# Weights requested ahead of the norms, eight norm tiles in flight, and keys turned sooner in a two-block network on one Trainium2 core

## The chip, the cores and the metric

One core of a Trainium2 chip runs the whole network in one program, in float32. The metric is the device time of one execution in microseconds, on the slowest core, which here is the only one. An execution's time is its profiled span and the start and end around it.

## The reference

x has 2 sequences of 2048 tokens and 128 channels. Four sublayers follow, each with a residual and a layer norm over the channels behind it:

```python
x = _layernorm(x + gated_delta(x))      # first mixer: 16 heads, keys 64 wide, values 128 wide
x = _layernorm(x + ffn_block(x))        # two layers of local attention and a gated feed forward
x = _layernorm(x + wkv_mixer(x))        # second mixer
x = _layernorm(x + ffn_block(x))

# inside the first mixer
q, k, v = (silu(causal_conv(x @ w, conv)) for w, conv in ...)      # 4 taps
q, k = q * rsqrt(sum(q * q) + 1e-6), k * rsqrt(sum(k * k) + 1e-6)  # per head
g = -exp(A_log) * softplus(x @ w_a + dt_bias);  beta = 2 * sigmoid(x @ w_b)
S = S * exp(g_t);  delta = (v_t - k_t @ S) * beta_t;  S = S + outer(k_t, delta);  o_t = (q_t / 8) @ S
y = o * rsqrt(mean(o * o) + eps) * norm_w * silu(x @ w_g);  return y @ w_out

# inside a layer of ffn_block
x = x + local_attention(rope(l2norm(q) * q_scale), rope(l2norm(k) * k_scale), v) @ wo
h = layernorm(shift_token(x)) * ln_g + ln_b
x = x + ((h @ w1a + b1a) * gelu(h @ w1g + b1g)) @ w2 + b2
```

## The kernel before

Activations lie with channels on the partitions, in three buffers (x0T, x1T, x2T), a sequence beside the other, each with 3 columns of zeros ahead. The program is a row of phases. Each phase is one or more blocks (`nc.Block()`): within one, every engine has its own instruction stream and waits on semaphores; at its end all engines, SyncE's stream too, come together. `phase_semaphores` clears a phase's semaphores on GpSimd in a block of its own, with lines at L83.

**gated_delta** (L150) takes a sequence in 16 chunks of 128 tokens, so 32 turns. A turn has named parts on each engine. `early`: projection of a and b, then projections 0 to 3 (the keys in 0 and 1, the queries in 2 and 3), 4 taps each, into PSUM banks 4 and 5 in turn; ScalarE copies each out with Silu (L491). VectorE does the scalar chain of the decays, `decays` (L570 to L585), and `norms`: sums of the squares that GpSimd made (L717), the multiplication by the inverse norms (L602) that GpSimd's power made (L724). GpSimd makes gV, four tiles (L720), as input to the cumulated log decays (TensorE L359). `mid`: sums and logs of the decays, then for the keys and after that the queries: eight turns through TensorE (L367), ScalarE's copy (L508), the 16 heads' products (L375). VectorE makes nA from the key products (L612), PT from the query products (L616). SyncE carries the diagonal blocks of nA to DRAM and back, VectorE inverts them, SyncE carries the inverses into Tm (L317 to L325). `late`: projections 4 to 7 (v), 8 to 11 (gate), products with the state, then three levels that merge the inverses (L381 turns Tm, L419 and L428), delta, output and state. `tail` turns y (L457) and projects it out (L463) into bank 7, and VectorE adds it to x (L684). Each engine runs these parts in the order `late(n)`, `early(n + 1)`, `tail(n)`, `mid(n + 1)`; each turn on TensorE ends with the products and the next begins with `early`.

**post_norm** (L1425) goes through the sequences in four rounds of two tiles of 128 x 512: sum or copy (L1484, L1486), mean by a product with ones (L1451), centring (L1489), squares (L1469), variance by one-column products (L1456), its scale (L1492), power on GpSimd (L1476), spreading (L1461), product (L1495). There are two PSUM banks for each of the two tiles.

**ffn_block** (L855) primes its semaphores (L831), loads the masks (L877) and copies them on GpSimd (L882), and runs both layers in a loop of the program: a block with 22 DMA requests of SyncE (L890 to L905), the multiplication of the rope table on VectorE (L916) and TensorE's wait for all weights; `attention_layer`; `feed_forward`. `build` runs post_norm, then copy_all (L2178), a copy of the normed activations for the residual, then ffn_block.

## Time and profile before

| | us |
|---|---|
| median of 3 runs (lowest, highest) | 6176.56 (6173.99, 6180.19) |
| the profiled execution | 6176.74 |
| its span | 6174.9 |
| TensorE busy | 5260.5 (85%) |
| VectorE busy | 3993.2 (65%) |
| ScalarE busy | 2818.8 (46%) |
| GpSimd busy | 2189.4 (35%) |
| mean granted TensorE clock | 0.911 of full |

The first mixer's turns run from about 67 to 3122 us, the first block from 3200 to 4134, the second mixer from 4187 to 5107, the second block from 5184 to 6110. Busy times overlap, since the engines run side by side; a releaser behind an idle time is what ended it. A clock of 1.00 is 2.4 GHz on TensorE, 0.50 is 1.2 GHz.

### The profile page before, as it was taken

The page shows a single profiled execution, that of the slowest core. Times are in us where ns is not written, and L with a number is a line of the kernel's source. Part 1 is how long each engine was busy: PE and PEld are TensorE (multiplying, and loading weights), DVE is VectorE, ACT ScalarE, POOL GpSimd, SP SyncE. Part 2 cuts the span into 40 slices and gives each one's busy share as a digit, 9 for nine tenths or more (in the row PEclk, how much of TensorE's full clock was granted, in tenths as well). Part 3 has the DMA queues.
Part 4 walks back from the last instruction along what each step waited for, and adds up shares of the span by engine and source line. Part 5 has one row for each costly group of instructions (what it writes and reads, how often), then busy time and mean ns, then how long its engine had stood idle before and what let it go on. Part 6 is the DMA issues. An engine that isn't in the chain of part 4 may idle for free. (4 is left out here: it accounts for less than half of the span.)

```text
span 6174.9 us, 107736 instructions
## 1 busy us (share of the span) xinstructions
PE 5260.5 (85%) x36898; PEld 3652.1 (59%) x36898; DVE 3993.2 (65%) x8920; ACT 2818.8 (46%) x6592; POOL 2189.4 (35%) x1545
## 2 busy tenths in 40 slices
PE   5999999999899999999959979985478775987988
PEld 3676776776667767667646635652156663654655
DVE  4655655556556565565549949944699545985983
ACT  1444444444444444344438838833400113874882
POOL 1323324333233233332326616603422113652650
PEclk7999999999999999999979989986699757998997
DMA  2000000000000000000000000000000000000000
GB/s 103 5 5 7 4 7 7 3 7 7 5 7 3 7 7 3 7 5 5 7 26 0 0 25 0 0 0 5 0 7 1 0 0 26 0 0 25 0 0 14
DMA packets 181374, 52.74 MB, mean 9 GB/s; under 512 B 151876, under 2 KB 177433, under 8 KB 180377
## 3 DMA queue, kind: packets, MB, share of 16 engines
q1 hardware_dynamic: 179880, 49.26, 3.5%
q10 hardware_dynamic: 1392, 2.20, 0.1%
q8 instruction: 55, 0.90, 0.1%
q14 instruction: 47, 0.38, 0.0%
HBM read 40.93 MB, written 10.49 MB: 8 GB/s over the span
## 5 line engine op out<-in xcount | busy, mean ns | idle before, releaser
L342 PE MATMUL gd_ps<-gd_taps,gd_xwin 128*128 128x512 f32 x2048 | 913.6, 605 | 0.0
L342 PEld LDWEIGHTS gd_ps<-gd_taps,gd_xwin 128*128 128x128 f32 x2048 | 391.9, 194 | 475.1 <-issue 472.9
L745 POOL TENSOR_TENSOR gd_o_rn<-gd_tmp,gd_mhalf 128x8 f32<-128x8 f32 x64 | 103.5, 1635 | 1189.8 <-DVE gd_tmp L670 1189.8
L522 ACT ACTIVATE gd_X<-gd_ps 128x512 f32<-128x512 f32 x512 | 267.8, 635 | 538.4 <-PE gd_ps L381 538.4
L1185 ACT ACTIVATE L_ffn_s<-L_ffn_s,L_ffn_nb,L_ffn_r 128x128 f32<-128x128 f32 x1024 | 408.0, 480 | 3.2
L647 DVE TENSOR_TENSOR gd_Z<-gd_ps,cst 128x256 f32<-128x256 f32 x384 | 163.1, 425 | 323.6 <-PE gd_ps L419 257.6
L1007 POOL TENSOR_TENSOR L_ffn_t<-L_ffn_t 128x512 f32<-128x512 f32 x128 | 162.4, 1268 | 541.5 <-DVE L_ffn_t L1224 541.5
L739 POOL TENSOR_TENSOR gd_gate<-gd_gate,gd_norm_w 128x2048 f32<-128x2048 f32 x32 | 145.1, 4535 | 588.1 <-ACT gd_gate L491 588.1
L491 ACT ACTIVATE gd_v<-gd_ps 128x512 f32<-128x512 f32 x128 | 76.4, 597 | 530.9 <-PE gd_ps L342 530.9
L381 PE MATMUL gd_ps<-cst,gd_gV 128*128 128x128 f32 x2048 | 269.6, 277 | 46.5 <-ACT gd_decay L517 46.5
L641 DVE SCALAR_TENSOR_TENSOR gd_v<-gd_ps,gd_n_ec,gd_v 128x128 f32<-128x128 f32 x512 | 135.2, 342 | 230.7 <-PE gd_ps L393 230.7
L1032 PE MATMUL L_ffn_ps<-L_ffn_sb_wqkv,L_ffn_hT 128*128 128x512 f32 x256 | 153.8, 684 | 144.5 <-ACT L_ffn_hT L1141 144.5
L381 PEld LDWEIGHTS gd_ps<-cst,gd_gV 128*128 128x128 f32 x2048 | 223.4, 142 | 77.6 <-ACT gd_decay L517 75.4
L602 DVE TENSOR_TENSOR gd_qk<-gd_qk,gd_r_norm 128x1024 f32<-128x1024 f32 x64 | 112.2, 1753 | 207.7 <-POOL gd_r_norm L724 207.7
L428 PE MATMUL gd_ps<-gd_Z,gd_X 128*128 128x64 f32 x2048 | 239.2, 275 | 0.0
L419 PE MATMUL gd_ps<-gd_gV,gd_nA 128*128 128x64 f32 x2048 | 235.8, 274 | 0.0
L428 PEld LDWEIGHTS gd_ps<-gd_Z,gd_X 128*128 128x128 f32 x2048 | 233.8, 192 | 0.0
L419 PEld LDWEIGHTS gd_ps<-gd_gV,gd_nA 128*128 128x128 f32 x2048 | 233.7, 192 | 0.0
L1016 POOL TENSOR_TENSOR L_ffn_r<-L_ffn_ss,L_ffn_mhalf 128x8 f32<-128x8 f32 x128 | 210.9, 1648 | 23.6 <-DVE L_ffn_ss L1256 23.6
L1075 PEld LDWEIGHTS L_ffn_ps<-L_ffn_kT,L_ffn_qT 64*64 64x64 f32 (+1 forms) x4096 | 149.0, 137 | 115.8 <-issue 100.9
L1086 PE MATMUL L_ffn_ps<-cst,L_ffn_s 128*128 128x128 f32 x1024 | 167.1, 286 | 58.4 <-ACT L_ffn_s L1185 58.4
L717 POOL TENSOR_TENSOR gd_scratch<-gd_qk 128x1024 f32<-128x1024 f32 x64 | 124.4, 1944 | 258.8 <-ACT gd_qk L491 258.8
(361 smaller groups left out, 13813.5 us busy)
## 6 DMA issues: line engine op xcount, KB each, us to landing
L_ffn_sb_rope<-in_rope SPq DMA_DIRECT2D x4, 2048.0 KB, 8.2
gd_tap_row<-in_L_attn_conv_v SPq DMA_DIRECT2D x2, 2048.0 KB, 6.8
gd_blocks<-gd_nA SPq DMA_DIRECT2D x256, 16.0 KB, 1.7
gd_Z<-gd_blocks SPq DMA_DIRECT2D x32, 128.0 KB, 2.0
gd_inverses<-gd_Z SPq DMA_DIRECT2D x32, 128.0 KB, 1.7
gd_gV<-gd_inverses SPq DMA_DIRECT2D x256, 16.0 KB, 1.9
L_ffn_sb_wqkv<-in_L_ffn_wqkv SPq DMA_DIRECT2D x4, 768.0 KB
gd_tap_row<-in_L_attn_conv_q SPq DMA_DIRECT2D x1, 2048.0 KB, 15.1
```

The costliest lines, as they stand in the source:

```text
L342: ins = pe.matmul(ps[4 + i % 2][:], xwin[:, t:t + P] if i < 8 else xwin[:, PAD:PAD + P], taps[:, t, 512 * SLICE[i]:512 * (SLICE[i] + 1)] i ...
L381: ins = pe.transpose(ps[4 + gi][:, P * k:P * (k + 1)], Tm[:, HG * gi + k], ident)
L419: ins = pe.matmul(ps[gi][:, 64 * k:64 * (k + 1)], nA[:, h], even(Tm, h, h + 1, s)[:, 0], start=True, stop=True)
L428: ins = pe.matmul(ps[gi][:, 64 * k:64 * (k + 1)], X[:, h], Z[:, h], start=True, stop=True)
L522: act.activation(heads(X, gi).rearrange("p h x -> p (h x)"), ps[4 + gi][:], ACT.Copy).then_inc(x_s.sem, 1)
L647: dve.tensor_tensor(heads(Z, gi), ps[gi][:, 0:256].rearrange("p (h x) -> p h x", h=HG), mask, ALU.mult).then_inc(z_s.sem, 1)
L1007: pool.tensor_tensor(t1[b][:, K], t1[b][:, K], t2[b][:, K], ALU.add).then_inc(la.k_sum.sem, 1)
L1016: pool.tensor_tensor(rq, ss[b][:, 0:AH], mhalf[:, 0:AH], ALU.pow).then_inc(la.r_q.sem, 1)
L1032: pe.matmul(ps_k[:], hT[b][:], wqkv[:, INNER:2 * INNER], start=True, stop=True).then_inc(la.k_mm.sem, 1)
L1075: ins = pe.matmul(ps_s[i][rows, P * k:P * (k + 1)], qT[b][half(i), k, rows], kT[b][half(i), k, WIN * wd:WIN * wd + P], start=True, stop=True)
L1086: ins = pe.transpose(ps_p[i][:, P * k:P * (k + 1)], s[b][:, i, k], ident)
L1185: ins = act.activation(s[b][:, i, k], s[b][:, i, k], ACT.Exp, scale=r[b][:, h:h + 1], bias=nb[b][:, i, k:k + 1])
```

## The change

In gated_delta TensorE turns the keys ahead of the decay sums, between the halves of the output's projection, and takes projection 4 between the query turns and the query products. ScalarE copies the keys ahead of the decays' exponentials. VectorE sums the key squares ahead of the decays and multiplies the keys ahead of the query sums. GpSimd takes the key power ahead of the query squares, the query power behind gV. In ffn_block the loads of layer 0 stand in a block ahead of the post norm, which is now called from within; the layer loop is unrolled; the next layer's rope, scales, wqkv and wo are requested in a block ahead of feed_forward, its w1, w2 and vectors beside the rope multiplication. post_norm has no loop: eight tiles, one PSUM bank each, all waits constants; it makes its constant and zeroes the pads on GpSimd, and ScalarE copies each finished tile to the second buffer where copy_all did.

```diff
@@ gated_delta, TensorE
+                def turn_qk(n, part):
+                    w((kn_s if part else qn_s).now(n))
+                    for q in range(2):
...
+                        w(proj_out.now(n, 2 + q) if m < 2 else t_out.now(n, q))
...
                 def late(n, b):
-                    for i in range(4, 12):
+                    for i in range(5, 12):
                         project(n, i)
...
+                def tail_and_mid(n):
+                    turn_y(n)
+                    output(n, range(0, G // 2))
+                    turn_qk(n + 1, 1)
+                    decay_sums(n + 1)
+                    output(n, range(G // 2, G))
+                    k_products(n + 1, 1)
+                    turn_qk(n + 1, 0)
+                    project(n + 1, 4)
+                    k_products(n + 1, 0)
@@ gated_delta, ScalarE
                 def mid(n):
+                    copy_qk(n, 1)
                     w(c_mm.now(n)); w(S_s.before(n))
                     act.activation(e_c[:], ps[6][:, 0:2 * H], ACT.Exp).then_inc(c_s.sem, 1)
...
+                    copy_qk(n, 0)
@@ gated_delta, VectorE
+                def norms_and_decays(n):
                     cn.start(n)
...
+                    square_sums(n, 0)
+                    decays(n)
+                    normed(n, 0)
+                    square_sums(n, 1)
                     cn.end()
...
+                    normed(n, 1)
@@ gated_delta, GpSimd
                 def early(n):
...
+                    squares_of(n, 0)
+                    inverse_norms(n, 0)
+                    squares_of(n, 1)
                     w(g_s.now(n))
...
+                    inverse_norms(n, 1)
@@ ffn_block
         with nc.Block() as block:
             @block.sync
             def _(sp):
+                load_attention(sp, 0)
                 sp.dma_start(masks[:, 0:2], A["masks"]).then_inc(la.f_const, 16)
...
+                load_feed_forward(sp, 0)
+
+        meanwhile()
+        la.prime(nc)
...
+        for layer in range(DEPTH):
+            with nc.Block() as block:
...
+                @block.sync
+                def _(sp):
+                    if layer:
+                        load_feed_forward(sp, layer)
...
+                    pe.wait_ge(la.w_loaded, (layer + 1) * (16 * 2))
...
+                    dve.tensor_tensor(rope[:], rope[:], scales[:].unsqueeze(1).to_broadcast([P, NC, 4, AD]), ALU.mult)
+
+            attention_layer(nc, cst, xo, xa, la, masks, rope, wqkv, wo, ps, layer * NC, f"{pre}{layer}")
 
             with nc.Block() as block:
                 @block.sync
                 def _(sp):
...
+                    if layer + 1 < DEPTH:
+                        load_attention(sp, layer + 1)
+                    sp.wait_ge(la.f_loaded, (layer + 1) * (16 * 13))
+
+            feed_forward(nc, cst, xa, xo, la, w1, w2, vecs, L, layer * (T // FW), f"{pre}{layer}")
@@ post_norm
+                for i in range(n):
+                    pe.wait_ge(summed, i + 1)
+                    pe.matmul(ps[i][:], ones, x[i][:], start=True, stop=True).then_inc(mean, 1)
+                for i in range(n):
+                    pe.wait_ge(squares, i + 1)
...
+                if also is not None:
+                    for i in range(n):
+                        act.wait_ge(done, i + 1)
+                        act.activation(also[:, at(i)], dst[:, at(i)], ACT.Copy)
@@ build
-            post_norm(nc, cst, [x1], x1, sems, "n1_")
         x2 = flat(activations("x2T"))
-        copy_all(nc, x2, x1)
         with phase_semaphores(nc) as sems:
-            ffn_block(nc, A, cst, "L0_ffn_", x2, x0, sems)
+            ffn_block(nc, A, cst, "L0_ffn_", x2, x0, sems, lambda: post_norm(nc, cst, [x1], x1, sems, "n1_", x2, [x2]))
```

`load_attention` requests the rope table, six rows of scales, wqkv and wo: 9 DMAs. `load_feed_forward` requests w1, w2 in three, and 9 vectors: 13 DMAs. `turn_y`, `output`, `decay_sums` and `k_products` hold the instructions of the old `tail` and `mid`.

## Rows read from the trace of the kernel before

**Rows 1.** Busy time by stretch: span, then each engine's, granted clock, DMA share, GB/s.

```profile
1041.80:1054.70 12.90, 8.34 (x81) 7.21 (x80) 10.09 (x22) 4.05 (x6) 12.90 (x11) 0.81 0.04 4
```

**Rows 2.** Timeline of one turn on TensorE: start, us, operation, tiles, idle before and releaser.

```profile
1018.64 13.98 PE L342 MATMUL gd_ps<-gd_taps,gd_xwin 128*128 128x512 f32 x32
...
1034.21 3.74 PE L463 MATMUL gd_ps<-gd_X,gd_w_out 128*128 128x128 f32 x32
...
1043.47 1.09 PE L367 MATMUL gd_ps<-cst,gd_qk 128*128 128x128 f32 x8 [1.64 <-DVE gd_qk L602]
1044.81 2.06 PE L375 MATMUL gd_ps<-gd_kT 64*128 64x128 f32 x32 [0.25 <-ACT gd_kT L508]
...
1050.62 4.15 PE L375 MATMUL gd_ps<-gd_qT,gd_kT 64*128 64x128 f32 x32 [2.22 <-DVE gd_nA L612]
1054.70 14.97 PE L342 MATMUL gd_ps<-gd_taps,gd_xwin 128*128 128x512 f32 x32
...
1077.40 0.66 PE L381 MATMUL gd_ps<-cst,gd_gV 128*128 128x128 f32 x4 [0.33 <-ACT gd_decay L517]
```

**Rows 3.** Timeline of the same turn, VectorE.

```profile
1021.01 0.18 DVE L564 COPY gd_e_ab<-gd_ab 128x16 f32<-128x16 f32 x1
...
1026.64 1.87 DVE L570 TENSOR_SCALAR gd_tmp<-gd_e_ab 128x16 f32<-128x16 f32 x1
...
1044.97 2.28 DVE L602 TENSOR_TENSOR gd_qk<-gd_qk,gd_r_norm 128x1024 f32<-128x1024 f32 x1 [1.64 <-POOL gd_r_norm L724]
...
1048.33 4.21 DVE L612 SCALAR_TENSOR_TENSOR gd_nA<-gd_ps,gd_n_beta,gd_decay 128x128 f32<-128x128 f32 x16
```

**Rows 4.** Timeline of GpSimd, the same turn and the next.

```profile
1020.76 3.23 POOL L745 TENSOR_TENSOR gd_o_rn<-gd_tmp,gd_mhalf 128x8 f32<-128x8 f32 x2 [37.17 <-DVE gd_tmp L670]
1026.47 2.00 POOL L717 TENSOR_TENSOR gd_scratch<-gd_qk 128x1024 f32<-128x1024 f32 x1 [2.48 <-ACT gd_qk L491]
...
1035.19 4.03 POOL L720 TENSOR_TENSOR gd_gV<-gd_g,cst 128x512 f32<-128x512 f32 x4
1039.18 5.76 POOL L724 TENSOR_TENSOR gd_r_norm<-gd_sq_sum,gd_mhalf 128x16 f32<-128x16 f32 x2
...
1134.36 5.76 POOL L724 TENSOR_TENSOR gd_r_norm<-gd_sq_sum,gd_mhalf 128x16 f32<-128x16 f32 x2
```

**Rows 5.** Timeline of SyncE's DMA requests, same turn; line L325 by itself, its landing times.

```profile
1068.44 3.75 SPq L325 DMA_DIRECT2D gd_gV<-gd_inverses  x8
...
DMA to landing us min/median/max: 1.7/1.9/3.1
```

**Rows 6.** Busy time by stretch: clock behind nA, and in the second mixer.

```profile
1050.60:1056.60 6.00, 5.98 (x35) 4.49 (x36) 4.72 (x13) 0.00 (x0) 4.29 (x6) 0.50 0.21 19
4506.50:4509.30 2.80, 0.00 (x0) 0.00 (x0) 2.80 (x4) 0.00 (x0) 0.00 (x0) 1.00 0.00 0
```

**Rows 7.** Stretches of norm 1 and norm 2, then norm 2's timeline.

```profile
3122.40:3162.20 39.80, 30.70 (x144) 22.82 (x144) 15.19 (x33) 5.04 (x8) 7.96 (x8) 0.79 0.00 0
...
4134.60:4181.80 47.20, 39.40 (x144) 28.09 (x144) 17.32 (x33) 5.04 (x8) 8.05 (x8) 0.58 0.00 0
...
4136.14 3.78 PE L1451 MATMUL n_ps<-n_x,cst 128*128 128x512 f32 x4 [2.86 <-DVE n_x L1484]
...
4143.10 3.76 PE L1461 MATMUL n_ps<-cst,n_rstd 128*128 128x128 f32 x16
```

**Rows 8.** Timeline of seams: into block one, between its layers; second mixer's loads.

```profile
3176.82 0.41 SPq L890 DMA_DIRECT2D L_ffn_sb_rope<-in_rope  x1
...
3189.22 4.42 DVE L916 TENSOR_TENSOR L_ffn_sb_rope<-L_ffn_sb_rope,L_ffn_sb_scales 128x4096 f32<-128x4096 f32 x1 [19.33 <-DMA L_ffn_sb_scales<-in_L_ffn_k_scale]
...
3200.14 2.07 PE L1032 MATMUL L_ffn_ps<-L_ffn_sb_wqkv,L_ffn_hT 128*128 128x512 f32 x2 [38.69 <-ACT L_ffn_hT L1141]
...
3679.14 2.07 PE L1032 MATMUL L_ffn_ps<-L_ffn_sb_wqkv,L_ffn_hT 128*128 128x512 f32 x2 [23.74 <-ACT L_ffn_hT L1141]
...
4197.53 1.85 SPq L1594 DMA_DIRECT2D wf_vec<-in_L_attn_time_maa  x4
```

More of the change, by code:

```diff
@@ L351, in early, with k_products, decay_sums @@
                         project(n, i)
-                def mid(n):
+                def turn_qk(n, part):
+                    w((kn_s if part else qn_s).now(n))
+                    for q in range(2):
+                        m = 2 * (1 - part) + q
+                        w(proj_out.now(n, 2 + q) if m < 2 else t_out.now(n, q))
+                        for k in range(4):
+                            first = H * part + 8 * q + 2 * k
+                            ins = pe.transpose(ps[4 + q][:, P * k:P * (k + 1)], qk[:, first:first + 2].rearrange("p h x -> p (h x)"), ident)
+                        ins.then_inc(t_mm.sem, 1)
+                def k_products(n, part):
+                    for g0 in range(0, G, 2):
+                        w(t_out.now(n, 2 * (1 - part) + g0 // 2))
+                        w(exp_s.now(n, g0 + 1) if part else nA_s.now(n, g0 + 1))
+                        for k in range(HG):
+                            for gi in (g0, g0 + 1):
+                                at = pair(HG * gi + k)
+                                ins = pe.matmul(bank(gi)[:, k], kT[half(gi), at], (kT if part else qT)[half(gi), at], start=True, stop=True)
+                                if k == HG - 1:
+                                    ins.then_inc((kk_mm if part else kq_mm).sem, 1)
+                def decay_sums(n):
                     w(g_s.now(n))
@@ L458, in tail, with output @@
                         ins.then_inc(yt_mm.sem, 1)
-                    for gi in range(G):
+                def output(n, groups):
+                    for gi in groups:
                         w(yT_s.now(n, gi))
@@ L689, in _ @@
                     early(b * NC)
-                    decays(b * NC)
-                    norms(b * NC)
+                    norms_and_decays(b * NC)
                     mid(b * NC)
@@ L888, in _ @@
+        la.prime(nc)
+        ps = [ctx.enter_context(nc.psum_tensor(f"{pre}ps{i}", [P, 512], F32)) for i in range(8)]
+        L = [ps[0:4], ps[4:8]]
+        for layer in range(DEPTH):
+            with nc.Block() as block:
+                @block.gpsimd
+                def _(pool):
+                    if layer == 0:
+                        pool.wait_ge(la.f_const, 16)
+                        pool.tensor_copy(masks[:, 2:NC], masks[:, 1:2].to_broadcast([P, NC - 2, P]))
                 @block.sync
@@ new lines, in _ @@
+                for i in range(n):
+                    pe.wait_ge(squares, i + 1)
+                    for j in range(FW // P):
+                        ins = pe.matmul(ps[i][:, j:j + 1], sq[i][:, P * j:P * (j + 1)], ones[:, 0:1], start=True, stop=True)
+                    ins.then_inc(var_mm, 1)
+                for i in range(n):
+                    pe.wait_ge(rstd_s, i + 1)
+                    for j in range(FW // P):
+                        ins = pe.matmul(ps[i][:, P * j:P * (j + 1)], rstd[i][:, j:j + 1].to_broadcast([P, P]), ident, start=True, stop=True)
+                    ins.then_inc(spread, 1)
@@ L1498 @@
+                for i in range(n):
+                    dve.wait_ge(var_mm, i + 1)
+                    dve.tensor_scalar(var[i][:], ps[i][:, 0:FW // P], 1.0 / D, EPS, ALU.mult, ALU.add).then_inc(var_s, 1)
+                for i in range(n):
+                    dve.wait_ge(spread, i + 1)
+                    dve.tensor_tensor(dst[:, at(i)], ps[i][:], x[i][:], ALU.mult).then_inc(done, 1)
 RH, RS = 16, 8
```

236 lines of the change are left out of this document (91 added, 145 removed).

## The prediction

> **What bounds the kernel now.** Read first the busy times of the page, then the stretches. TensorE is busy 85% of the span, but no engine fills it, so each stage is read for what its last wait is. About half the span is the first mixer: 32 turns, one every 95.18 us (GpSimd's power for the inverse norms starts at 1039.18 and again at 1134.36 [rows 4]). I set T = 0 where a turn's projections begin on TensorE, 1018.4. Nearly everything in a turn is TensorE back to back; its stops stand together, between T 23.4 and T 36.3: 1.64 us for the normed keys, 0.25 for their copy, a short one for the normed queries, 2.22 for nA [rows 2], and the products behind nA take 4.15 us where the same 32 matmuls took 2.06 [rows 2]. In the 12.9 us of that stretch TensorE is busy 8.34, at a granted clock of 0.81 of full [rows 1]: the clock fell to 0.50 in the stop for nA and stayed there 6 us into the work behind it [rows 6]. That is why the projections behind it take 14.97 us where the ones of the turn's start took 13.98 [rows 2]. Outside the mixer the waste is at the seams: the four post norms last 39.8 to 47.2 us each for some 8 us of power on GpSimd and 15 to 17 of VectorE [rows 7], and between a norm and the first attention matmul TensorE stands 38.69 us (some 6 less in the second block, with fewer semaphores to clear), between the two layers of a block 23.74 [rows 8].
>
> **The first mixer, walked once through with the new order.** All starts are from rows; full clock is assumed first.
> VectorE and GpSimd, keys: the second key projection is out at T 8.0, since GpSimd's squares begin at T 8.07 and take 2.0 [rows 4], to T 10.1. VectorE, done with the gated output at 8.24, sums them (1.22) and adds, to 11.5. GpSimd's power takes 2.9 (5.76 for two [rows 4]), to 14.5. Meanwhile VectorE runs the decay chain. It took 5.8 from 1026.64: 19 instructions of some 0.2 us, and ahead of them L570 with 1.87 where a copy of the same size took 0.18; it ended with GpSimd's squares (1028.5) [rows 3, 4]. Without that it is 4.1 us; but its last two small instructions now meet the query squares on GpSimd (14.9 to 16.9) and the first gV tile (1.0 [rows 4]), so I take its end at T 18.0. The keys' multiplication then meets the next gV tile: 2.28 us like the one of row 1044.97 [rows 3], to T 20.3. Today the keys are there at T 24.9.
> TensorE: projections to 14.0, y turned to 15.8, half of the output 1.8 (half of 3.74 [rows 2]), to 17.6. It waits for the keys to T 20.4, 2.8 us: longer than today's 1.64. Then key turn 1.1, sums 0.6, logs 3.7 (8 of the 512-column matmuls, whose 32 took 13.98), second half of the output 1.8, key products 1.9: T 29.3. Query turn to 30.4, a copy, **project 4** 3.4 (13.98 / 4), to 34.1, query products 2.0, to T 36.1. Today TensorE is at T 36.3 then, without project 4. So 7 projections less: the rest, from 1054.70 to 1077.07 (1077.40 less its 0.33) less 3.43 and less the 1.0 lost to the clock, is 17.9, and the level 0 turn could start at T 54.3 instead of 59.0 [rows 2].
> What is late next is the **round trip of the inverse**. nA: query sums 1.2 plus a wait for a gV tile, power to 25.4, queries multiplied to 27.9 (2.28 again), output added, n_ec behind a GpSimd tile to 29.1, nA 4.21 [rows 3], to T 33.3 against 34.1 today. From its end to the last block's landing it is 21.5 us today (nA ends 1052.5 [rows 3]; its last DMAs are requested by 1068.44 + 3.75 and land 1.9 later [rows 5]). That gives T 54.8, so it, not TensorE, sets the start: 54.9 against 59.0, a gain of 4.1 us a turn. Project 4, moved into the wait for nA, thus earns nothing beyond what nA's own earliness allows; ahead of it stand only TensorE's own products, and ScalarE copies v in the same order as before.
> Clock: the new stop of 2.8 us is one piece with full work on both sides. In the second mixer a like stop of 2.8 us held 1.00 all through; today's 2.22 behind the shorter ones ends at 0.50 [rows 6]. If it drops, key turn, sums and logs run some 6 us at half clock, 2.8 us are lost, the key products and nA slip to T 35.4, and the gain is 1.9. I take the middle of the two, 3.0, since the rows show one case that held and one that didn't: 30 turns x 3.0 = 90. The first turn of each sequence has no output to put in between and its decays now wait behind the key squares; project 4 fills the wait for nA: 3 us each, 6. Sum **96**; bounds 30 x 1.9 and 30 x 4.1, so 60 to 130.
>
> The Trainium skill, "SBUF — State Buffer", section "SBUF: two separate sides", says that VectorE and GpSimd take a shared port pair as an exclusive lock for a whole instruction. The blocked L570 agrees with it. Taken strictly it speaks against this change, since the decays now run beside the key power; that is rival 3.
>
> **The post norms.** Work is the same, eight tiles at once instead of four rounds of two. At half clock a pair costs TensorE 3.78 for the means, 3.2 for the variances (4143.10 less the end of the means), 3.76 for spreading [rows 7]: 5.4 a tile, 43 for eight; at full clock half of that, some 22. VectorE (17) and GpSimd (8) fit beneath either. TensorE in one dense run after a cold start came back after 6 us [rows 6], but the one-column variances may lose it again (in the four norms the clock averages 0.79 and 0.58 [rows 7]). I take 34 with head and tail; bounds 26 and 46. That is 6 less for norms 1 and 3 (39.8, the third 41.8) and 14 less for 2 and 4 (47.2, the fourth 47.0): **40**, bounds -6 and 72. What is late next in it is TensorE itself; power beside it costs nothing.
>
> **Loads and seams.** Blocks end with all engines together (SyncE's first rope request stands behind GpSimd's mask copy), so SyncE's requests in a block of their own aren't hidden by the norm; only their landing is. Entering, today: 12.4 us from the rope request to the multiplication (3189.22) [rows 8] plus some 8 for the copy of the activations and the masks. After: 23 requests, 0.46 each as in L1594's four in 1.85 [rows 8], a little more for the six broadcast ones, 11.6; then, after the norm, 0.8 for the last tile's second copy on ScalarE, the multiplication 4.42, and the rest unchanged. 38.7 becomes 30.5, and the second entry gains as much: **16** together. Between layers: the 23.74 hold 11.5 us of requests before the multiplication; after, 13 requests (6.1) beside the 4.42, so 12.2, but 9 requests (5.6 with their block) now stand alone ahead of the feed forward, and the last block's wait costs 0.6 and a cold start about 1: 4 x 2 = **8**. Bound from below 0 for both (if requests stay at the 0.6 to 0.8 us that the same ones take now), 35 from above. The layer loop unrolled: attention and feed forward keep their inner loops, bounded by the few register instructions that it saves and at worst some code loading at each seam, +-5; I take 0.
>
> **Sum**: against the profiled execution's 6176.7 (span 6174.9; the median of three runs is 6176.6, the same): 96 + 40 + 24 = 160, so **6017 us**.
>
> **Rivals.** (1) The clock holds: no drop in the turns (4.1 x 30 + 7 = 130) and norms at 26 (28 + 42 = 70): 224 off, 5953. For it: the 2.8 us stop that held [rows 6]. Against: each turn drops once today.
> (2) The clock falls every turn and norms run at half clock: 62 for the mixer, 0 for the norms, 24 for the seams: 6091. For it: the norms' 0.58.
> (3) Power holds the port: L570 waits to T 14.5, the chain then meets squares and two gV tiles, keys come at 22.3, the stop is 4.7 and surely cold: about 1 us a turn is left, 33 + 64: 6080. Against it: L564, a copy from and to SBUF, took 0.18 beside a power on GpSimd [rows 3, 4].
> (4) Slower: the round trip from nA rules and nA slips. Everything that GpSimd does between (power of the queries behind gV, masks of the decays behind that) is in one queue, and VectorE's small instructions wait in it tile by tile. With 21.6 behind nA, each us that it ends later than T 37.4 (59.0 less 21.6) makes a turn a us longer than today. It outweighs the 64 of the norms and seams from 2.1 us on, that is nA beyond T 39.5, 6.2 later than worked out; at T 41.4 a turn is 99.2 us and the kernel 6176.7 + 30 x 4.0 - 64 = 6233. For it: the waits for GpSimd's tiles in the walk, of up to 1.2 us each, are guesses, and several stand one behind the other. Against: nA's inputs are all sooner, and these waits are counted already.
> (5) The change does little: the keys' gain is eaten by the new stop and the norms don't overlap: within 0.2% of today.
>
> **How the numbers follow.** Forecast 0.50 (6017, its own range 5985 to 6050), (1) 0.17, (2) 0.13, (3) 0.11, (4) 0.04, (5) 0.05. Below 5948 and above 6092 I leave some 2 in 10 or less, with (4) and (5) outside. 0.2% (12 us) is about what a measurement can tell: faster 0.91, same 0.05, slower 0.04.
>
> **What would show it.** A turn's period of 91 to 93 us in GpSimd's power row; TensorE's stop for the keys 1.7 to 3 us, the one for nA gone, level 0 turn waiting for the DMA of the inverse rather than for ScalarE; the granted clock behind the keys' stop; each norm 26 to 40 us with TensorE's means in one run; rope multiplied with no wait for a DMA; requests 0.45 us apart. The forecast is wrong if nA ends no sooner against the turn's start, or if a seam is longer than today.

## The result, and the profile after

The changed kernel takes **5926.6 us** (median of 4 runs, 5919.5 to 5931.8). The ratio to the kernel before, measured beside it, is 0.9594 (95% interval 0.9579 to 0.9609): 251 us saved where 160 were forecast, and 21 us below the 5948 under which (with 6092 above) the prediction left at most 2 in 10. Its profiled execution has a span of 5917.7 us against 6174.9, 257.2 less. The first lines of its page, with the granted clock in 40 slices:

```profile
span 5917.7 us, 106596 instructions
...
PE 5154.2 (87%) x36898; PEld 3594.3 (61%) x36898; DVE 3964.4 (67%) x8910; ACT 2823.5 (48%) x6606; POOL 2226.4 (38%) x1555
...
PEclk8999999999999999999989989986699657998998
```

Stage by stage, in the two traces:

| stage | before | after | saved | forecast |
|---|---|---|---|---|
| first mixer, first projection to last output | 3054.7 | 2891.1 | 163.6 | 96 |
| four post norms | 39.8, 47.2, 41.8, 47.0 | 28.2, 29.4, 27.6, 27.9 | 62.7 | 40 |
| all the rest (entries, between the layers, written-out loop) | | | 30.9 | 24 |
| span | 6174.9 | 5917.7 | 257.2 | 160 |

**One turn of the mixer on TensorE** (timeline; T = 0 is 1054.15; the rows answer to [rows 2]):

```profile
1054.15 0.41 PE L349 MATMUL gd_ps<-gd_w_ab,gd_xwin 128*128 128x32 f32 x2
1054.40 13.98 PE L342 MATMUL gd_ps<-gd_taps,gd_xwin 128*128 128x512 f32 x32
...
1069.96 1.95 PE L468 MATMUL gd_ps<-gd_X,gd_w_out 128*128 128x128 f32 x16
1073.27 1.09 PE L360 MATMUL gd_ps<-cst,gd_qk 128*128 128x128 f32 x8 [1.36 <-DVE gd_qk L629]
...
1074.56 3.68 PE L380 MATMUL gd_ps<-gd_gV,cst 128*128 128x512 f32 x8
...
1083.29 3.70 PE L342 MATMUL gd_ps<-gd_taps,gd_xwin 128*128 128x512 f32 x8 [0.25 <-ACT gd_qT L528]
1086.92 2.06 PE L370 MATMUL gd_ps<-gd_qT,gd_kT 64*128 64x128 f32 x32
1088.90 10.57 PE L342 MATMUL gd_ps<-gd_taps,gd_xwin 128*128 128x512 f32 x24
...
1107.75 1.14 PE L384 MATMUL gd_ps<-cst,gd_gV 128*128 128x128 f32 x8 [0.88 <-DMA gd_gV<-gd_inverses]
```

The stop for nA is gone, the query products take 2.06 us instead of 4.15, and the level 0 turn (1107.75) starts at T 53.6 instead of 59.0. What it waits for there is the DMA of the inverse, as forecast. The stop for the keys is 1.36 us, shorter than before and half of the 2.8 forecast.

**The same turn on VectorE** (answers to [rows 3]): the last two small instructions of the decays, the keys' multiplication, the queries', nA.

```profile
1069.37 1.64 DVE L613 TENSOR_SCALAR gd_n_beta<-gd_tmp 128x16 f32<-128x16 f32 x1
1071.05 0.96 DVE L614 TENSOR_SCALAR gd_beta<-gd_tmp 128x16 f32<-128x16 f32 x1
1071.93 1.21 DVE L629 TENSOR_TENSOR gd_qk<-gd_qk,gd_r_norm 128x1024 f32<-128x1024 f32 x1
...
1078.93 2.28 DVE L629 TENSOR_TENSOR gd_qk<-gd_qk,gd_r_norm 128x1024 f32<-128x1024 f32 x1 [3.86 <-POOL gd_r_norm L756]
...
1082.28 4.22 DVE L648 SCALAR_TENSOR_TENSOR gd_nA<-gd_ps,gd_n_beta,gd_decay 128x128 f32<-128x128 f32 x16
```

**And on GpSimd** (answers to [rows 4]), with the next turn's power, 89.25 us later:

```profile
1065.76 2.90 POOL L756 TENSOR_TENSOR gd_r_norm<-gd_sq_sum,gd_mhalf 128x16 f32<-128x16 f32 x1 [1.54 <-DVE gd_sq_sum L624]
1069.09 1.90 POOL L751 TENSOR_TENSOR gd_scratch<-gd_qk 128x1024 f32<-128x1024 f32 x1 [0.42 <-ACT gd_qk L516]
1070.94 5.09 POOL L764 TENSOR_TENSOR gd_gV<-gd_g,cst 128x512 f32<-128x512 f32 x4
1076.00 2.90 POOL L756 TENSOR_TENSOR gd_r_norm<-gd_sq_sum,gd_mhalf 128x16 f32<-128x16 f32 x1
...
1155.01 2.90 POOL L756 TENSOR_TENSOR gd_r_norm<-gd_sq_sum,gd_mhalf 128x16 f32<-128x16 f32 x1 [1.54 <-DVE gd_sq_sum L624]
```

The keys' multiplication took 1.21 us: it did not wait for a gV tile. GpSimd waited for it: four gV tiles took 5.09 us where they had taken 4.03 [rows 4].

**Busy time by stretch** (span; busy time of PE, PEld, DVE, ACT, POOL; granted clock; DMA share; GB/s): behind the keys' stop, where the products of the queries run (answers to [rows 1, 6]), norm 1 and norm 2 [rows 7].

```profile
1072.00:1078.00 6.00, 4.73 (x20) 2.90 (x21) 3.03 (x4) 4.01 (x7) 6.00 (x4) 1.00 0.00 0
1084.00:1090.00 6.00, 6.00 (x42) 3.45 (x42) 4.39 (x14) 1.62 (x2) 4.86 (x6) 1.00 0.18 16
2980.24:3008.39 28.15, 26.94 (x144) 21.53 (x144) 15.05 (x32) 9.46 (x15) 8.01 (x11) 0.79 0.02 2
3940.49:3969.85 29.36, 27.88 (x144) 22.93 (x144) 16.70 (x32) 4.88 (x8) 7.97 (x9) 0.77 0.00 1
```

The clock is at its full level (2.4 GHz) behind the keys' stop and where it had been at half (1.2 GHz) before. In the norms it is on average 0.79 and 0.77: as high as norm 1 had before, well above norm 2's 0.58.

**The seams** (timeline, answers to [rows 8]): first and last request ahead of norm 1, the first attention matmul, the first matmul of the feed forward, the first of the second layer.

```profile
2964.68 0.40 SPq L915 DMA_DIRECT2D L_ffn_sb_rope<-in_rope  x1
...
2977.17 2.52 SPq L932 DMA_DIRECT2D L_ffn_sb_vecs<-in_L_ffn_b  x6
...
3019.22 2.08 PE L1090 MATMUL L_ffn_ps<-L_ffn_sb_wqkv,L_ffn_0hT 128*128 128x512 f32 x2 [11.56 <-ACT L_ffn_0hT L1199]
...
3379.38 1.22 PE L1415 MATMUL L_ffn_ps<-L_ffn_0f_h,cst 128*128 128x512 f32 x1 [10.16 <-ACT L_ffn_0f_h L1449]
...
3488.46 2.07 PE L1090 MATMUL L_ffn_ps<-L_ffn_sb_wqkv,L_ffn_1hT 128*128 128x512 f32 x2 [10.41 <-ACT L_ffn_1hT L1199]
```

The 23 requests take 15.0 us (2964.68 to 2979.69) in a block in which no engine computes. TensorE's idle time between norm and attention is 11.56 instead of 38.69, between the layers 10.41 instead of 23.74; but it is 10.16 ahead of the feed forward, where it was 3.96.

### The profile page after: what moved, and what is told of

It is laid out like the page before. It is cut to its first block and busy times, and to the rows that moved or that the text cites. A ratio compares the mean times of both kernels' runs of the same rounds, so it can differ in the third digit from the quotient of the medians.

```text
span 5917.7 us, 106596 instructions
## 1 busy us (share of the span) xinstructions
PE 5154.2 (87%) x36898; PEld 3594.3 (61%) x36898; DVE 3964.4 (67%) x8910; ACT 2823.5 (48%) x6606; POOL 2226.4 (38%) x1555
## 5 line engine op out<-in xcount | busy, mean ns | idle before, releaser
L1243 ACT ACTIVATE L_ffn_0s<-L_ffn_0s,L_ffn_0nb,L_ffn_0r 128x128 f32<-128x128 f32 x512 | 204.0, 480 | 1.6
L1243 ACT ACTIVATE L_ffn_1s<-L_ffn_1s,L_ffn_1nb,L_ffn_1r 128x128 f32<-128x128 f32 x512 | 204.0, 480 | 1.6
L756 POOL TENSOR_TENSOR gd_r_norm<-gd_sq_sum,gd_mhalf 128x16 f32<-128x16 f32 x64 | 185.6, 2899 | 49.5 <-DVE gd_sq_sum L624 49.3
L516 ACT ACTIVATE gd_qk<-gd_ps 128x512 f32<-128x512 f32 x128 | 76.5, 598 | 259.3 <-PE gd_ps L342 259.0
L771 POOL TENSOR_TENSOR gd_decay<-gd_decay,cst 128x512 f32<-128x512 f32 x128 | 190.0, 1515 | 0.0
L691 DVE TENSOR_TENSOR gd_gV<-gd_ps,gd_gV 128x256 f32<-128x256 f32 x256 | 108.7, 425 | 120.0 <-PE gd_ps L431 120.0
L1065 POOL TENSOR_TENSOR L_ffn_1t<-L_ffn_1t 128x512 f32<-128x512 f32 x64 | 81.2, 1268 | 259.6 <-DVE L_ffn_1t L1282 259.6
```

The costliest lines, as they stand in the source:

```text
L516: act.activation(dst, src, ACT.Silu).then_inc(proj_out.sem, 1)
L756: pool.tensor_tensor(r_norm[:, first:first + H], sq_sum[:, first:first + H], mhalf[:, 0:H], ALU.pow).then_inc(rn_s.sem, 1)
L771: pool.tensor_tensor(heads(decay, gi), heads(decay, gi), cst[:, C_UPTO:C_UPTO + P].unsqueeze(1).to_broadcast([P, HG, P]), ALU.mult).then_i ...
L1243: ins = act.activation(s[b][:, i, k], s[b][:, i, k], ACT.Exp, scale=r[b][:, h:h + 1], bias=nb[b][:, i, k:k + 1])
```

## The experiments

Each kernel ran beside the kernel before; its ratio to that is the number to compare. "At 6176.6" is the ratio times the time before. The span is that of the one execution that was profiled: for output_first it was the slowest of four (5902 to 5922 us), for the changed kernel the fastest, so spans alone don't rank these two.

| kernel | ratio (95% interval) | at 6176.6 | span |
|---|---|---|---|
| changed | 0.9594 (0.9579 to 0.9609) | 5926 | 5917.7 |
| mixer_alone | 0.9727 (0.9711 to 0.9744) | 6008 | 6012.9 |
| norms_alone | 0.9884 (0.9864 to 0.9903) | 6105 | 6112.3 |
| unrolled_alone | 0.9969 (0.9957 to 0.9982) | 6157 | 6167.5 |
| loads_back | 0.9621 (0.9607 to 0.9634) | 5943 | 5948.2 |
| power_behind | 1.0009 (1.0000 to 1.0019) | 6182 | 6186.9 |
| keys_delayed_one | 0.9813 (0.9797 to 0.9829) | 6061 | 6057.5 |
| keys_delayed | 0.9862 (0.9846 to 0.9879) | 6091 | 6100.5 |
| projection_back | 0.9796 (0.9777 to 0.9814) | 6051 | 6034.6 |
| output_first | 0.9553 (0.9537 to 0.9569) | 5901 | 5920.1 |
| two_queues | 0.9588 (0.9572 to 0.9604) | 5922 | 5929.4 |
| seams_more | 0.9518 (0.9502 to 0.9533) | 5879 | 5873.8 |
| both_more | 0.9474 (0.9458 to 0.9490) | 5852 | 5852.5 |

### Where the time came from: four kernels with parts of the change

**mixer_alone.** The kernel before with `gated_delta` of the changed one, whole; nothing else of the diff.

> The kernel before with only the first mixer of the changed kernel. If the changed kernel's trace can be read stage by stage, the mixer is worth what it shortened there: 5.9 us a turn (95.18 to 89.25) and 163.6 us from its first projection to its last output, so about 6013 us (6008 to 6020). By the prediction's 3.0 a turn it would be 6081.

Measured 6008, span 162.0 us less. Its turns are those of the changed kernel (89.2 us each). The 163.6 read from the changed trace is the mixer's own.

**norms_alone.** The kernel before with the new `post_norm` at the old places.

> The kernel before with only the post norm's function of the changed kernel, called at the old places and with the old copies behind it. If the norms are worth what the changed trace shows (28.2, 29.4, 27.6, 27.9 us where the old ones took 39.8, 47.2, 41.8, 47.0), 63 us are saved: about 6114 (6106 to 6122). By the prediction's 40 it would be 6137. If a norm in one dense run is only fast because of the loads ahead of it, less than 40.

Measured 6105 (6093 to 6117), span 62.6 less. The norms' gain is their own too, and needs no loads ahead of them. Which of the function's changes (eight tiles at once, one bank each, no loop) earns how much was not separated.

**unrolled_alone.**

```diff
-        with nc.Fori(0, DEPTH) as layer:
-            one = bass.ds(layer, 1)
+        for layer in range(DEPTH):
+            one = slice(layer, layer + 1)
```

> The kernel before with only its loop over the two layers of a block written out: same loads at the same places, same norms, same mixer. The prediction put this at 0 (within 5): 6172 to 6182. The changed trace has each attention layer 3 to 3.6 us shorter and weights requested closer together; if that comes from the register arithmetic of the layer number in waits and addresses, 4 x 3.3 for the attention plus some 8 for the requests are saved: about 6156 (6148 to 6165).

By the ratio 19 us (11 to 27), by the spans 7.4: more than the 0 of the prediction, and near its ±5 by the span alone. In the two profiled executions the part behind the first mixer is 13 us shorter; the mixer, whose code is the same, happened to end 5.5 us later. The expectation's reading, each attention layer 3 to 3.6 us shorter, doesn't hold. On TensorE, from their first matmul to the idle time ahead of the feed forward, the four took 351.5, 348.6, 350.8 and 350.2 us here against 353.6, 351.3, 350.0 and 349.6 before, so two are shorter and two longer. What is shorter at all four is the idle time ahead of the attention, 36.22, 22.56, 30.38 and 21.90 against 38.69, 23.74, 32.80 and 24.32: 8.5 us together.

**loads_back.** Mixer, norm and written-out loop of the changed kernel, with loads, copies and the clearing of pads as before.

> The changed kernel without its new places for the loads: mixer, post norm and written-out layer loop of the changed kernel on the kernel before, with the loads, the copies and the clearing of the pads where they were. The three parts alone were worth 2.73, 1.16 and 0.31%, together 4.2% against 4.06% of the whole change, so by the sum of the parts the loads are worth nothing or cost a little: 5917 to 5927. By the traces they are worth 6 at each entry and some 6 between the layers of each block, 24 in all: 5946 to 5952.

Measured 5946.3 as it ran, 5943 by the ratio (0.9621): near the second number, so the loads' new places are worth something: 17 us by the ratios (0.27%, with intervals that just overlap), 30 by the spans, of which 4 lie in the mixer, whose code is the same. The sum of the three parts' ratios (4.2%) overshot the 3.8% measured here; they share one set of runs of the kernel before, whose median was 6186.5, some 8 us above those beside the changed kernel and loads_back (6177.9 and 6179.0), and each carries that. (The set beside power_behind, keys_delayed, projection_back and output_first has 6185.9 too.) The spans add up better: 162.0 + 62.6 + 7.4 = 232.0 for the three, 226.7 for them together.

### What the mixer's gain hangs on

**power_behind.** The keys' power behind gV on GpSimd, as before; the order on VectorE and TensorE as changed.

```diff
                 def early(n):
                     squares_of(n, 0)
-                    inverse_norms(n, 0)
                     squares_of(n, 1)
...
+                    inverse_norms(n, 0)
                     inverse_norms(n, 1)
```

> The changed kernel with the keys' power behind the gV tiles on GpSimd again, everything else as changed. Theory: the keys' multiplication is what the front of the turn hangs on. Squares to T 16.9, gV to about T 21, power to T 24, keys by T 25 to 26.3 instead of 19.0; TensorE stops 7 us for them, nA and the level 0 turn come 6 to 7 later, the clock falls: 5927 + 30 x 6 to 9, so 6110 to 6200. Rival: the order on TensorE and VectorE is what earns the gain and the power's place is worth 1 or 2 us a turn: 5950 to 5990.

Ratio 1.0009. The rest of the change still saves its 82 us (4.06 less 2.73%), so the mixer is some 88 us *slower* than before; by the traces it is 105 (3045.8 against 2941.2 us from the first to the last power of the gated output). The row of the keys' turn:

```profile
1169.04 1.97 PE L360 MATMUL gd_ps<-cst,gd_qk 128*128 128x128 f32 x8 [7.32 <-DVE gd_qk L629]
```

A stop of 7.32 us, and the turn behind it takes 1.97 where 1.09 is the full clock's. Turns take 97.0 to 98.5 us. The new order puts the keys ahead of everything, so it is only as good as the keys are early, and the place of one GpSimd instruction of 2.90 us is worth more than the whole gain of the mixer.

**keys_delayed and keys_delayed_one.** More work on VectorE between the decays and the keys' multiplication. The kernel that ran as keys_delayed had two such sums (2.46 us), not the one that its expectation names; keys_delayed_one has one.

```diff
                     decays(n)
+                    for _ in range(2):
+                        cn.link(dve.tensor_reduce(pause[:, H:2 * H], scratch[:].rearrange("p h (two x) -> p (h two) x", two=2)[:, H:2 * H], AX_X, ALU.add))
                     normed(n, 0)
```

> The changed kernel with one more sum over the keys' squares (1.21 us on VectorE, its result unused) ahead of the keys' multiplication. It makes the stop for the keys what the prediction took it for: 2.6 us if the multiplication still takes 1.21, 3.6 if it now meets a gV tile and takes 2.28. If the clock holds through such a stop, nA is as much later and a turn grows by 1.3 to 2.3: 5966 to 5997. If the clock falls in it, as it did in the stop of 2.22 before, some 2.8 more a turn: 6045 to 6080.

> The changed kernel with really one more sum (1.22 us on VectorE) ahead of the keys' multiplication; keys_delayed had two of them, 2.46 us, its stop for the keys was 4.28 us, and behind it the turn and the logs ran at half clock. Here the stop should be 2.6 to 3.1, the size that the prediction took it for (2.8) and could not settle. If the clock holds at that size, nA is 1.2 to 1.7 later and a turn grows by as much: 5927 + 30 x 1.2 to 1.7, so 5963 to 5978. If it falls, some 2.8 a turn more: 6047 to 6062. The turn's key row 1.97 (half clock) or 1.09 (full) tells it directly.

keys_delayed_one on TensorE, its extra sum and its multiplication on VectorE, and the stretch behind the stop:

```profile
1118.26 1.88 PE L361 MATMUL gd_ps<-cst,gd_qk 128*128 128x128 f32 x8 [3.27 <-DVE gd_qk L630]
...
1120.65 4.24 PE L381 MATMUL gd_ps<-gd_gV,cst 128*128 128x512 f32 x8
```

```profile
1115.00 1.20 DVE L636 TENSOR_REDUCE gd_pause<-gd_scratch 128x16 f32<-128x1024 f32 x1
1116.24 1.89 DVE L630 TENSOR_TENSOR gd_qk<-gd_qk,gd_r_norm 128x1024 f32<-128x1024 f32 x1
```

```profile
1118.00:1122.00 4.00, 3.74 (x14) 3.15 (x15) 1.43 (x3) 2.20 (x3) 3.48 (x2) 0.57 0.00 0
```

Here the multiplication does wait for a gV tile (1.89). The stop is 3.27 us, 1.9 longer than in the changed kernel, and the clock is down right behind it: 0.57, against 1.00. For 1.2 us of work the kernel is 135 us longer (0.9813 against 0.9594), some 4.3 a turn: 1.9 the stop, 2.4 the clock. With two sums the stop is 4.28 and the turns 93.8 to 95.5, as long as before the change.

What about the 2.8 us of the forecast, between these two? No run has that stop in the turns. Stops of some 2.4 us are in the traces, and they come out either way. The second turn of a sequence has one even in the changed kernel, where the clock held both times; in mixer_alone, the same mixer at nearly the same time, it fell the first time and held the second:

```profile
180.84 1.09 PE L360 MATMUL gd_ps<-cst,gd_qk 128*128 128x128 f32 x8 [2.36 <-DVE gd_qk L629]
```

```profile
180.83 1.65 PE L360 MATMUL gd_ps<-cst,gd_qk 128*128 128x128 f32 x8 [2.35 <-DVE gd_qk L629]
```

In the kernel before, the second mixer's idle time of 2.93 us (2.8 of it in [rows 6]) had a clock of 1.00 behind it too. So 1.36 us held and 3.27 fell in every steady turn that was read; in between, the length of the stop alone doesn't decide, and what does stays open.

The Trainium skill, "TensorE: Matmul & The Clock Gate", section "HAM oscillation — how this bites in real kernels", describes the same pattern, a wait in every round of a loop that sends each next round off at half clock. The pair above agrees with it (0.57 against 1.00).

**projection_back.** Project 4 is back among the later projections.

```diff
                 def tail_and_mid(n):
...
                     turn_qk(n + 1, 0)
-                    project(n + 1, 4)
                     k_products(n + 1, 0)
```

> The changed kernel with the fifth projection back among the later ones, so that TensorE has nothing between the query turn and the query products. The prediction said that moving it earns nothing of its own, since the inverse's round trip sets the start of the level 0 turn: then 5927, with a stop of about 3.4 us for nA and the wait of 0.88 for the DMA gone. Worked out from the changed trace: TensorE would come to the level 0 turn at T 52.7 + 3.4 = 56.2 instead of 53.6, 2.6 us later a turn, so 5927 + 78 = 6005 with the clock held, and some 1.8 a turn more, 6060, if the stop of 3.4 us lets the clock fall.

```profile
1206.05 1.16 PE L370 MATMUL gd_ps<-gd_qT,gd_kT 64*128 64x128 f32 x16 [1.54 <-DVE gd_nA L646]
1208.12 2.08 PE L370 MATMUL gd_ps<-gd_qT,gd_kT 64*128 64x128 f32 x16 [0.91 <-DVE gd_nA L646]
1210.13 16.20 PE L342 MATMUL gd_ps<-gd_taps,gd_xwin 128*128 128x512 f32 x32
```

The wait for nA is back, 2.45 us in two pieces, and in this turn the clock falls in it (the 32 matmuls take 16.20 us instead of 13.98). It doesn't in every turn. Another one of the same trace, with the same wait, keeps its clock:

```profile
655.54 1.16 PE L370 MATMUL gd_ps<-gd_qT,gd_kT 64*128 64x128 f32 x16 [1.54 <-DVE gd_nA L646]
657.61 1.16 PE L370 MATMUL gd_ps<-gd_qT,gd_kT 64*128 64x128 f32 x16 [0.90 <-DVE gd_nA L646]
658.70 14.00 PE L342 MATMUL gd_ps<-gd_taps,gd_xwin 128*128 128x512 f32 x32
```

The trace has this wait in 28 turns. In ten of them the clock stays at 1.00 and the turn lasts 91.5 us: 2.3 more than the 89.2 of the changed kernel, which is TensorE coming late by itself. In the other eighteen it falls and they last 93.0 to 94.6. The kernel is 125 us longer, three quarters of what the mixer gained (2.0 of 2.7%). The shares of single moves don't add up to that gain: taking back the keys' power alone cost more than all of it.

**output_first.** Both halves of the output ahead of the keys' turn.

```diff
                     turn_y(n)
-                    output(n, range(0, G // 2))
+                    output(n, range(G))
                     turn_qk(n + 1, 1)
                     decay_sums(n + 1)
-                    output(n, range(G // 2, G))
```

> The changed kernel with both halves of the output ahead of the keys' turn. TensorE then comes to the keys at T 19.6, behind them (T 19.0), so the stop of 1.36 is gone, and the key products follow on the logs. If the round trip of the inverse behind nA sets the turn, and nA waits for VectorE and GpSimd's masks rather than for the key products, nothing changes: 5920 to 5935. If the split is what brings nA sooner, a turn grows by 0.6: 5945.

```profile
1163.60 1.04 PE L360 MATMUL gd_ps<-cst,gd_qk 128*128 128x128 f32 x8
...
1197.84 1.52 PE L384 MATMUL gd_ps<-cst,gd_gV 128*128 128x128 f32 x12 [1.59 <-DMA gd_gV<-gd_inverses]
```

The stop for the keys is gone, nA starts 16.52 us after the keys' power as in the changed kernel (1172.35 less 1155.83; 1082.28 less 1065.76): the key products, 1.6 sooner by the same measure, don't bring it forward. TensorE is only longer idle in front of the DMA, 1.59 instead of 0.88. Yet the turns take 88.5 instead of 89.2, and the kernel is 25 us faster (0.9553 against 0.9594, intervals apart; 18 by the medians as they ran, 21 by 31 turns), which neither theory gave. TensorE's last products before the level 0 turn end sooner, so ScalarE copies the state's output sooner, and the stops for those copies between the groups of the turn (0.38 twice in the changed kernel) shrink to one of 0.30. So splitting the output, which the prediction had counted as a part of the gain, costs a little.

### The two bounds of the level 0 turn, and the exposed requests

**two_queues.** The 16 requests of the inverse's round trip shared between SyncE (4 and 5) and ScalarE (4 and 3); on ScalarE:

```diff
                 def late(n):
+                    w(nA_s.now(n))
+                    for q in range(4, NB):
+                        act.dma_start(blocks_dram[q].rearrange("h k m -> k h m"), diagonal(nA, q)).then_inc(blk_out.sem, 16)
                     for i in range(4, 12):
                         project(n, i)
+                    w(Tm_zero.now(n)); w(inv_out.now(n))
+                    for q in range(5, NB):
+                        act.dma_start(diagonal(Tm, q), inverse_dram[q].rearrange("h i j -> i h j")).then_inc(T_in.sem, 16)
```

> The changed kernel with the 16 requests of the inverse's round trip shared between SyncE and ScalarE (4 + 4 out, 5 + 3 back). If the round trip behind nA sets the level 0 turn, it comes 1.9 sooner for the first four and 1.3 for the second; the wait of 0.88 for the DMA goes. But output_first showed that ScalarE's four copies of the state's output (4.25 us, each ahead of one group's turn) stand close behind: stops of 4 x 0.33 to 0.38 come instead of 0.88 + 0.38 + 0.38, so only 0.2 to 0.3 a turn: 5917 to 5921. If the round trip is all of it, 0.88 a turn: 5900. If ScalarE's requests delay its copies of v and the gates, slower than 5927.

```profile
1108.78 0.66 PE L384 MATMUL gd_ps<-cst,gd_gV 128*128 128x128 f32 x4 [0.33 <-ACT gd_decay L552]
1109.81 0.66 PE L384 MATMUL gd_ps<-cst,gd_gV 128*128 128x128 f32 x4 [0.38 <-ACT gd_decay L552]
```

The wait for the DMA is gone and four stops for ScalarE stand in its place. The turns stay at 89.2 and the time is the same within the measurement (0.9588 against 0.9594). Round trip and ScalarE's copies end within some tenths of each other; removing one alone gives nothing.

**seams_more.** Every load is requested inside a block that computes: post norm, attention and feed forward each get a stream on SyncE that calls what is passed to them, and the feed forward's engines wait for its weights themselves.

```diff
-        with nc.Block() as block:
-            @block.sync
-            def _(sp):
+        def loads(sp):
...
-        meanwhile()
+        meanwhile(loads)
...
-            attention_layer(nc, cst, xo, xa, la, masks, rope, wqkv, wo, ps, layer * NC, f"{pre}{layer}")
+            attention_layer(nc, cst, xo, xa, la, masks, rope, wqkv, wo, ps, layer * NC, f"{pre}{layer}", (lambda sp: load_feed_forward(sp, 1)) if layer else None)
...
-            feed_forward(nc, cst, xa, xo, la, w1, w2, vecs, L, layer * (T // FW), f"{pre}{layer}")
+            feed_forward(nc, cst, xa, xo, la, w1, w2, vecs, L, layer * (T // FW), f"{pre}{layer}", (layer + 1) * (16 * 13), (lambda sp: load_attention(sp, 1)) if layer == 0 else None)
```

> The changed kernel with every load requested by SyncE inside a block that computes: the first layer's 23 inside the post norm's block, the next layer's 9 inside the feed forward's, its 13 inside the attention's; no block holds requests alone. The theory is that in the changed kernel requests in a block of their own are wholly exposed (15.0 us ahead of each block's norm, 5.9 ahead of each first feed forward): 2 x 15.0 + 2 x 5.9 + 2 x 3 between the layers, some 48 saved, so 5879 (5870 to 5890). The rival, that the weights' transfers then hold up the norm, gives back part: 5895 to 5915.

```profile
2968.28 9.07 PE L1508 MATMUL n_ps<-n_x,cst 128*128 128x512 f32 x16 [6.50 <-DVE n_x L1547]
...
3359.55 3.78 PE L1412 MATMUL L_ffn_ps<-L_ffn_0f_h,cst 128*128 128x512 f32 x4 [3.89 <-ACT L_ffn_0f_h L1447]
...
3466.87 2.07 PE L1081 MATMUL L_ffn_ps<-L_ffn_sb_wqkv,L_ffn_1hT 128*128 128x512 f32 x2 [8.74 <-ACT L_ffn_1hT L1190]
```

47 us (0.9518 against 0.9594), as worked out. TensorE stands 6.50 us ahead of the norm instead of 22.01, 3.89 ahead of the feed forward instead of 10.16, and the norm with the loads landing in it took no longer (the means 9.07 against 9.39). Here a request cost next to nothing where another engine had work in the same block, and its whole time where none had.

**both_more.** seams_more, output_first and two_queues together, and on VectorE nA ahead of n_ec and of the output's addition:

```diff
-                        tail(n, b, c)
-                        mid(n + 1)
+                        mid(n + 1, lambda: tail(n, b, c))
```

> seams_more, and in the mixer the two queues, the whole output ahead of the keys' turn (18 us in output_first), and on VectorE nA ahead of the output's addition and of n_ec (it starts 1.1 us sooner, but GpSimd's masks hold its last group to 0.7). Round trip and ScalarE's copies both sooner: 0.7 + 0.4 to 0.8 a turn below the changed kernel's 89.2, so 88.0 and with the seams 5845 (5830 to 5860). If nA's four groups then wait for the masks so that VectorE's order earns nothing, 5865.

5852 (0.9474): the fastest kernel here, 74 us below the changed one. The turns take 88.5 us, which is output_first's number: with both the DMA and nA sooner, the level 0 turn waits for ScalarE's copies in all four groups.

```profile
1186.72 0.66 PE L384 MATMUL gd_ps<-cst,gd_gV 128*128 128x128 f32 x4 [0.33 <-ACT gd_decay L551]
```

So VectorE's new order and the second queue gave nothing in the turns, and the state's output with those copies behind it is the next bound by the trace; no run shortened it.

## Why the prediction was wrong, step by step

The direction and each mechanism named (keys sooner, wait for nA filled, inverse's round trip next, norms bound by TensorE, requests exposed) were there. The sizes were too small, the mixer's above all: 163.6 against 96, that is 67.6 of the 97 by which the span was missed.

**A turn, worked again with what was measured.** The forecast had 4.1 us a turn at full clock and took 3.0. The turn shown gained 5.93 (95.18 to 89.25):
- *The clock, 1.1 us a turn.* "I take the middle of the two, 3.0, since the rows show one case that held and one that didn't." The middle was between the two outcomes of a stop of 2.8 us. The stop was 1.36 and the clock held in the steady turns. To leave the clock open was right for a stop near that size: those of 2.4 held in some turns and fell in others. The step that failed stands before it: "The keys' multiplication then meets the next gV tile: 2.28 us". The decays ended at T 17.9, as forecast (18.0), with both small instructions blocked as forecast (1.64 and 0.96 us). But the multiplication stood right behind them in VectorE's queue, started when the first gV tile ended, and the second tile waited for it. That is 1.07 of the 1.44 us by which the stop was missed; the rest is the starts of the multiplication and of the stop, off by some 0.2 each. keys_delayed_one shows what a longer stop does: multiplication 1.89, stop 3.27, clock at half, 4.3 a turn. It is 0.5 beyond the 2.8 forecast, so what that one would have cost isn't shown.
- *nA 0.95 us sooner* (ends at 1086.50, T 32.35, forecast 33.3). Not through the keys: output_first and the changed kernel have nA at the same distance from the keys' power although the key products differ by 1.6. It follows GpSimd's queue (query squares, gV, the queries' power, T 24.75 where 25.4 was forecast) and the queries' multiplication behind it, which did take 2.28 and ended 0.84 sooner than forecast.
- *The round trip 0.35 shorter* (21.25 from nA's end to the level 0 turn; 21.6 forecast).
- *0.54 behind the level 0 turn.* The forecast ended at that turn's start. But its four groups had also stopped for ScalarE before, 1.46 us in all (the first of them in [rows 2]); now the wait for the DMA covers part of that, and turn and first level products are 3.04 us apart instead of 3.58.
- *0.88 the other way.* 95.18 was one turn. The powers of the gated output (GpSimd) at the first and the last turn of each sequence, before and after, give the mean:

```profile
169.26 3.23 POOL L745 TENSOR_TENSOR gd_o_rn<-gd_tmp,gd_mhalf 128x8 f32<-128x8 f32 x2 [37.18 <-DVE gd_tmp L670]
...
1587.37 3.24 POOL L745 TENSOR_TENSOR gd_o_rn<-gd_tmp,gd_mhalf 128x8 f32<-128x8 f32 x2 [37.40 <-DVE gd_tmp L670]
```

```profile
163.08 3.24 POOL L787 TENSOR_TENSOR gd_o_rn<-gd_tmp,gd_mhalf 128x8 f32<-128x8 f32 x2 [37.52 <-DVE gd_tmp L706]
...
1502.72 3.24 POOL L787 TENSOR_TENSOR gd_o_rn<-gd_tmp,gd_mhalf 128x8 f32<-128x8 f32 x2 [37.40 <-DVE gd_tmp L706]
```

Fifteen turns apart: 94.54 and 89.31; over both sequences 94.42 and 89.37. Before, the turns went from 93.3 to 95.4, as long as the clock stayed down in each; after, nearly all are 89.2. The turn that was walked was among the long ones.

4.1 + 0.95 + 0.35 + 0.54 - 0.88 = 5.06, measured 5.05; times 30 is 151.5, and the first turns and the change of sequence gave 12.1 where 6 were forecast: 163.6. The upper bound of the range had only the clock in it (30 x 4.1). None of the walked starts had a bound of its own, and three of them erred to the same side.

**"Project 4 ... earns nothing beyond what nA's own earliness allows."** Wrong as a statement of what the move is worth, though the sum of 4.1 has the move in it. projection_back costs 125 us. The sentence set it against the round trip alone. Without it TensorE, which comes to the level 0 turn only 0.88 ahead, would come some 2.6 behind (3.43 less 0.88; 2.3 in the turns at full clock), and its wait for nA drops the clock in most turns. The same walk had the number: the level 0 turn "could start at T 54.3" with project 4 moved, so some 57.7 without.

**The split of the output** was walked and counted in, without asking what the unsplit order gives. It gives 25 us more.

**The post norms**, 62.7 against 40. "I take 34 with head and tail; bounds 26 and 46", where the work was 22 at full and 43 at half clock. Measured 27.6 to 29.4, TensorE busy nearly throughout. The step that failed is this term, mis-sized: 43 us of work at half clock is 43 x 0.5 / 0.79 = 27.2 at a clock of 0.79, which norm 1 had shown [rows 7] and the new norms have (0.79 and 0.77). The prediction had that row and used it for the doubt only. It could not know that norms 2 and 4 would rise to the same clock: with their 0.58 the same working gives 37. That the one-column variances lose the clock again was right: it was at half from 2995 to 3002 in norm 1 and for ten microseconds in norm 2. That is in the 0.79 and 0.77 already.

**Entries**, 16 forecast, some 12.6 measured (18.0 and 20.4 with the norms' 11.6 and 14.2 in them). The 23 requests took 15.0 rather than 11.6 us (the broadcast of a scale 2.08, the masks 2.26, where 0.46 was taken), and the multiplication of rope 5.93 rather than 4.42, beside GpSimd's copy of the masks. **Between the layers** 7 and 8 in the two blocks, forecast 4 each: the requests beside the multiplication took 5.5 us instead of 6.1 and were done soon after it, and it no longer waits for the rope table's load; the 9 ahead of the feed forward cost 6.2 and 6.1, close to the 5.6 worked out, and their empty block 0.3 in the second layers. **The written-out loop**: 0 taken, 7 to 19 measured, of which the traces show 8.5 in the idle time ahead of the attention.

**Rival 1** (clock holds) was the nearest with 5953. Its condition came true in the mixer, for another reason than it gave: it counted on a stop of 2.8 us that holds, and the stop was 1.36. Rival 3 (power holds the port) fell: the decays ran at 0.17 to 0.25 us an instruction beside it. Rival 4's chain, nA and then the round trip, is what rules now, at T 32.35 instead of the 37.4 from which it would have cost.

## What to carry to other kernels

When a wait is moved rather than removed, size the new stop with care: here 1.36 us cost itself, 3.27 cost itself and some 2.4 us a turn more by the clock, and stops of 2.4 went either way from one turn to the next. So one turn's rows don't tell what a stop costs: read the periods of all turns. For a loop, take the mean period from the first and last row of many turns before walking one of them, give every walked start a bound, and follow the walk past the instruction that is moved to the next one that waits. Work at an unknown clock is scaled with the mean clocks of the nearest rows (here 0.79 and 0.58, so 27 and 37 us) rather than put between full and half.

## What the runs showed of the hardware

**Who waits at the shared port depends on who stands ready when it comes free.** Against GpSimd's gV tiles of 128x512 the multiplication of 128x1024 took 1.21 (GpSimd's four tiles then 5.09 instead of 4.03) and 1.89 us, against its equally large tiles of the decays' masks 2.28. The Trainium skill, "SBUF — State Buffer", section "Who interferes with whom", says that the order of issue decides who blocks; these rows agree.

**GpSimd's power doesn't block VectorE.** In the changed kernel 14 small VectorE instructions of 0.17 to 0.25 us started inside the 2.90 us of the power that starts at 1065.76, though several of them have two inputs in SBUF and the power reads SBUF. The same page's rule (section "SBUF: two separate sides"), that the one that starts first has the pair for its whole instruction, would have held them until 1068.66. The measurement decides: the rule doesn't hold for this instruction, while it does for the squares beside it (L613, 1.64 us instead of 0.17).

**A stop of 2.4 us takes TensorE's clock down in some turns and not in others.** In projection_back the same wait of 2.45 us left the clock at 1.00 in ten of 28 turns, and in the other eighteen it fell, with the same instructions on both sides. In the changed kernel one of 2.36 held twice, in mixer_alone one of 2.35 fell once and held once.
